# Splitting loaded pairs into a high and a low part: four raw buffers and two low buffers in place of six shared ones

## The reference

```python
# layer 0
h = tanh(concat([X, t], 1) @ W1 + b1);  XB = X @ B.T
x = layernorm(x + h @ W2 + b2 + adj @ XB - rowsum(adj) * XB)
# layer 1: Chebyshev terms, T1 = adj x, T_next = 2 (adj T_curr) - T_prev, three products with adj
x = layernorm(x + x @ w[0] + T1 @ w[1] + T2 @ w[2] + T3 @ w[3] + bias)
# layer 2
z = concat([x, (adj @ x + x) / deg], 1) @ W + b;  out = relu(z) / norm(relu(z))
x = layernorm(x + out)
# layer 3: each row's last 100 nonzeros, weighted by 2**-(number of later nonzeros)
x = layernorm(x + w(adj != 0) @ (x @ weight) + bias)
```

## Time and profile before

| | before |
|---|---|
| median of 3 runs | 3085.93 us |
| the profiled execution | 3082.01 us |
| its span | 3080.2 us |
| TensorE busy | 2934.1 us (95%) |
| VectorE busy | 2831.4 us (92%) |
| ScalarE busy | 2353.7 us (76%) |
| share of the 16 DMA engines taken by SP's queue | 94.6% |
| data moved | 1148.18 MB, 373 GB/s on the mean |
| granted clock, mean | 0.992 |

### The profile page before, as it was taken

One profiled execution on the slowest core, in us unless ns is written; L12 is line 12 of the kernel. 1 busy time (PEld: TensorE's weight loads), 2 busy tenths in 40 slices (PEclk: granted clock), 3 DMA queues, 4 the chain that ended last, 5 costly groups with the idle time before them and its releaser, 6 DMA issues.

```text
span 3080.2 us, 35223 instructions
## 1 busy us (share of the span) xinstructions
PE 2934.1 (95%) x13425; PEld 2164.8 (70%) x13488; DVE 2831.4 (92%) x2407; ACT 2353.7 (76%) x1619; POOL 13.2 (0%) x31
## 2 busy tenths in 40 slices
PE   7999999999999998999989999998889999999998
PEld 6767778787788886888867888776766555555554
DVE  7999988988998889988899988999999999999997
ACT  5787877777777678776777776877777888888887
POOL 0000000000000000000000000000000000000000
PEclk9999999999999999999999999999999999999999
DMA  9999988999999999999999999989999999999996
GB/s 339 388 395 382 387 352 343 369 361 359 370 394 382 377 374 399 387 386 378 377 369 374 382 375 379 377 328 349 373 405 405 359 385 385 377 389 377 388 386 251
DMA packets 159015, 1148.18 MB, mean 373 GB/s; under 512 B 18160, under 2 KB 18336, under 8 KB 19584
## 3 DMA queue, kind: packets, MB, share of 16 engines
q1 hardware_dynamic: 157312, 1143.02, 94.6%
q0 software_dynamic: 1088, 2.48, 0.2%
q10 hardware_dynamic: 448, 0.43, 0.0%
HBM read 1143.75 MB, written 2.10 MB: 372 GB/s over the span
## 4 chain that ended last, share of the span: by engine, by line
PE 66%; DVE 23%; DMA 5%; ACT 3%; issue 2%; ACTq 0%; DVEq 0%
PE ACC L887 26%; DVE lo L626 17%; PE ACC L894 15%; PE ACC L1003 14%; DMA raw<-in_at 5%; PE PST L1017 4%; PE PSF L1017 3%; ACT hi L444 2%; PE PST L910 1%; DVE SV L737 1%; PE PSF L960 1%; DVE M L641 1%; PE PSF L967 0%; PE PSF L983 0%; PE PSF L963 0%
## 5 line engine op out<-in xcount | busy, mean ns | idle before, releaser
L626 DVE TENSOR_TENSOR lo<-raw,hi 128x2048 fp32r<-128x2048 f32 x832 | 1876.4, 2287 | 140.0 <-ACT hi L444 136.2
L444 ACT CAST hi<-raw 128x2048 fp32r<-128x2048 f32 x832 | 1584.7, 1912 | 526.2 <-PE ACC L887 338.4
L887 PE MATMUL ACC<-hi,T 128*128 128x512 f32 x4992 | 1280.6, 393 | 4.5 <-ACT hi L444 2.8
L887 PEld LDWEIGHTS ACC<-hi,T 128*128 128x128 f32 x4992 | 936.0, 189 | 207.6 <-issue 3.9
L894 PE MATMUL ACC<-lo,T 128*128 128x512 f32 x3200 | 887.4, 399 | 103.4 <-DVE lo L626 96.9
L894 PEld LDWEIGHTS ACC<-lo,T 128*128 128x128 f32 x3200 | 589.5, 189 | 298.4 <-DVE lo L626 183.9
L641 DVE SCALAR_TENSOR_TENSOR M<-raw,M 128x512 bf16<-128x512 f32 x1008 | 637.1, 687 | 40.9 <-PE ACC L1003 24.2
L450 ACT ACTIVATE Wf<-ACC,w_bias 128x1024 fp32r<-128x1024 f32 x512 | 568.1, 1114 | 128.5 <-PE ACC L1003 127.9
L1003 PE MATMUL ACC<-M,rank_b 128*128 128x512 bf16 x1969 | 518.3, 382 | 12.2 <-ACT Wf L450 6.7
L1003 PEld LDWEIGHTS ACC<-M,rank_b 128*128 128x128 bf16 x2032 | 158.8, 98 | 266.5 <-issue 131.2
L1017 PE MATMUL PST<-Wf,S 128*128 128x512 f32 x512 | 209.3, 489 | 0.0
(11 more groups left out here) (156 smaller groups left out, 1004.8 us busy)
## 6 DMA issues: line engine op xcount, KB each, us to landing
raw<-in_at SPq DMA_DIRECT2D x1088, 1024.0 KB, 6.8
SV<-in_x_cols SPq DMA_DIRECT2D x8, 256.0 KB, 10.1
out<-O POOLq DMA_DIRECT2D x7, 256.0 KB, 6.9
out<-O ACTq DMA_DIRECT2D x1, 256.0 KB, 2.0
w_sb<-in_w POOLq DMA_DIRECT2D x3, 64.0 KB, 9.6
bias<-in_bias_rows ACTq DMA_DIRECT2D x1, 128.0 KB, 11.8
l1w_sb<-in_l_w POOLq DMA_DIRECT2D x2, 64.0 KB, 8.4
rank_f<-in_rank_mats POOLq DMA_DIRECT2D x1, 128.0 KB, 10.2
```

Source lines behind the costliest of these rows:

```text
L444: nc.scalar.copy(hi[:, c % NH], raw[:, c % NR]).then_inc(hi_done, 1)
L626: tt(lo[:, c % NR], raw[:, c % NR], hi[:, c % NH].bitcast(f32), ALU.subtract).then_inc(lo_done, 1)
L887: ins = mm(acc[:, part], w, hi[:, p.c % NH, s, part], start=p.opens and s == 0 and i == 0, stop=False)
```

## The change

`lo` gets two buffers of its own, and `raw` is cut from six to four; the bytes are the same (six places of 8 KB per partition). A raw pair is given back once the low part has been made: SP waits for `lo_done` of pair c before it loads pair c + 4. VectorE, before it writes the low part of pair c, waits until TensorE is done with the low part of pair c - 2. In the counting pass the raw ring has four places as well.

```diff
-    NR = 6
+    NR = 4
+    NL = 2
...
-    raw, raw_at = place("raw", [P, NR, 2, BLK], f32)
-    lo, _ = place("lo", [P, NR, 2, BLK], f32r, raw_at)
+    raw, _ = place("raw", [P, NR, 2, BLK], f32)
+    lo, _ = place("lo", [P, NL, 2, BLK], f32r)
...
                 if 0 <= before < n_pairs:
-                    sp.wait_ge(pair_done, before + 1)
+                    sp.wait_ge(lo_done, before + 1)
...
                 dve.wait_ge(hi_done, c + 1)
-                tt(lo[:, c % NR], raw[:, c % NR], hi[:, c % NH].bitcast(f32), ALU.subtract).then_inc(lo_done, 1)
+                if c >= NL:
+                    dve.wait_ge(pair_done, c - NL + 1)
+                tt(lo[:, c % NL], raw[:, c % NR], hi[:, c % NH].bitcast(f32), ALU.subtract).then_inc(lo_done, 1)
...
-                        ins = mm(acc[:, part], ws[s][0], lo[:, p.c % NR, s, part], start=False, stop=p.closes and s == 1)
+                        ins = mm(acc[:, part], ws[s][0], lo[:, p.c % NL, s, part], start=False, stop=p.closes and s == 1)
```

## The result

The changed kernel takes 3275.94 us (median of four runs, 3260.26 to 3286.52), the kernel before 3084.29 us in the same comparison: a ratio of 1.062 (95% interval 1.060 to 1.064). Forecast were 3156 us and a range up to 3235. The direction was right; the 70 us that were forecast on top of the kernel before are little more than a third of the 192 measured. The profiled execution has a span of 3258.4 us, 178 more than before.

What follows compares the result with a forecast made beforehand. No single bound: TensorE, VectorE and DMA take turns, sharing the pipeline through the ring. Terms 28 + 8 + 18 + 8 + 9 + 1 = 72 us on 3082 give 3154, plus half of 4 us: 3156 us; range 3105 to 3235.

Steps and rivals of the forecast that it cites:

- Part 1, product 1: Row ends of product 1: the subtraction held up by `comb` makes `fin_a` 5.1 us late; 8 x 3.5 = 28 us.
- Part 1, the other products: Added wait of `split_lo` at row ends: zero in products 2 to 4, 1 us a row or 8 us in product 5.
- Part 2: Shorter raw ring, losses at row ends: 18 us in products 2 to 4, 8 in product 1, 9 in product 5.
- a steady stream fits in four places: Streaming pairs: four places allow a pair each 2.28 us and loads need 2.49, so nothing is lost there.
- almost the full rate: P groups of product 3, 1343 to 1545 us: landing median 5.0 us, cited against the rival of slower loads.
- The one with the loads as the bound throughout: Rival: landings stay at 6.8 or 8.6 us, 384 pairs at about 3.0 us, +135, about 3245 us; chance 0.12.
- fewer loads out make a shorter queue: Against the loads rival: landings of 8.6 us are queue time; median from issue to landing falls from 6.8 towards 5 us.
- No change: Rival: steady sums stream without loss and ends of rows are absorbed; 3083 to 3089 us; chance 0.05.
- faster: Rival: earlier ring release starts the next load 4.4 us earlier in eight rows, 35 us less, 3051 us; chance 0.03.
- The start: Start of the kernel: four loads go out at once and not six; 1 us.
- the counting pass: Counting pass: place reuse after 8.4 us against a landing of 4.8, so four places cover it; 0, upper end 10 us.
- The rule to double-buffer: Skill's advice, read for `lo`: two buffers are enough, the added wait is free everywhere, the sum 36 us less.

Runs made afterwards that it cites:

- low wait alone: Kernel before, six shared places, plus one VectorE wait: the subtraction of pair c waits until TensorE has ended pair c - 2; 3145.82 us, ratio 1.020.
- reach of four alone: Kernel before, six shared places, SP holding back the load of pair c until the subtraction of pair c - 4 (counting pass: its count); 3215.07 us, ratio 1.043.
- loads-alone kernel: Kernel without matmuls and steps, streaming 1 MB loads in sections of 120; with cast and subtraction 2.80 us per load at a reach of four, 2.50 at five.

## Why the prediction was wrong in size

**Part 1, product 1: right.** The same place in the changed kernel (VectorE, then TensorE, timeline):

```profile
321.30 2.29 DVE L629 TENSOR_TENSOR lo<-raw,hi 128x2048 fp32r<-128x2048 f32 x1 [0.16 <-ACT hi L445]
328.61 2.29 DVE L629 TENSOR_TENSOR lo<-raw,hi 128x2048 fp32r<-128x2048 f32 x1 [5.02 <-PE ACC L897]
330.82 0.16 DVE L681 COPY RS<-PSF 128x8 f32<-128x8 f32 x1
...
341.82 4.49 DVE L629 TENSOR_TENSOR lo<-raw,hi 128x2048 fp32r<-128x2048 f32 x2
...
319.31 1.07 PE L897 MATMUL ACC<-lo,T 128*128 128x512 f32 x4
```

Pair 98 ends at 320.38, and `fin_a` starts 10.4 us after it; before it was 296.66 - 291.32 = 5.3. That is 5.1 us late, as forecast. The subtraction after `fin_b` starts 21.4 us after that end, 18.2 before: 3.2 late, forecast 3.3. With the low wait alone TensorE's matmuls with that pair are 3.1 us late. Eight rows at 3.5 us were to give 28; with the low wait alone the seven rows that end before product 1's last one cost between 2.7 and 4.1 us each, and product 1 took 25 us more.

**Part 1, the other products: too low.** Products 2 to 4 were forecast at zero, "`comb` is short (under 2 us) and the row work comes later", and gave 21 us; product 5 at 8 and gave 17. In the row of product 5 that was read, the first wait with the low wait alone is 2.51 us, as forecast (2.5). Then the later waits were to take 1.5 us of it. Instead the delay of TensorE's matmuls grew from 1.7 to 4.9 us within three pairs. Most of that growth is TensorE itself. Before, and then with the low wait alone, the same work reads (the last line is a stretch; columns as in the earlier trace rows):

```profile
2071.44 2.00 PE L983 MATMUL PSF<-l3w_sb,TT 64*128 64x64 f32 x16
2073.37 1.19 PE L887 MATMUL ACC<-hi,T 128*128 128x512 f32 x4
2074.40 1.08 PE L894 MATMUL ACC<-lo,T 128*128 128x512 f32 x4
...
2122.43 1.20 PE L896 MATMUL ACC<-lo,T 128*128 128x512 f32 x4 [1.43 <-DVE lo L628]
2123.56 3.11 PE L985 MATMUL PSF<-l3w_sb,TT 64*128 64x64 f32 x16
2126.59 2.07 PE L889 MATMUL ACC<-hi,T 128*128 128x512 f32 x4
2128.47 1.91 PE L896 MATMUL ACC<-lo,T 128*128 128x512 f32 x4
...
2124.00:2131.00 7.00, 7.00 (x24) 5.94 (x24) 3.89 (x4) 3.48 (x4) 0.00 (x0) 0.51 0.73 269
```

After a pause of 1.43 us for the late subtraction the granted clock is at the lower of its two levels (1.2 GHz in place of 2.4), and the three steps take 2.8 us longer. So a small pause of TensorE can cost more than itself if the clock falls with it; that it was this pause that brought it down isn't shown.

**A term that the prediction left out: TensorE's clock.** The mean granted clock is 0.992 before, 0.987 with the low wait alone, 0.991 with the reach of four alone and 0.984 with the change. With two levels that is about 50, 80, 60 and 105 us at the lower one. Work takes about twice as long there (1.91 us in place of 1.08 above), so the additional time at the lower level can have cost at most half of itself: 16 us of the low wait's 64, 5 us of the reach's 133 and 28 us of the 178 in the change's profile. How much of that it did cost wasn't separated.

**Part 2 is the step that failed.** It was to give 35 us and gave 133, and not only the size was wrong but the mechanism: the cost was to arise at the ends of rows alone, and the loads themselves became slower. (In its sum 8 x 1.2 is 9.6 and not 9, which changes nothing.) The failing sentence is that a steady stream fits in four places, with the loads at 2.49 (or 2.65) us each. The rows read could not carry it: 2.49 us was read where loads had about three in flight (a median of 8.6 us from issue to landing), and it was used for a ring that lets a load be out for 4 x 2.49 - 4.3 = 5.7 us, a little over two loads. The loads-alone kernel gives 2.80 us there. At 2.80 us each the 832 pairs alone make 2330 us, by estimate, of the 2355 that the products took before, so almost nothing is left to hide the work at the ends of rows. The traces bear that floor out: from cast to cast over 20 pairs, half of all such stretches ran below 2.80 us per pair before, and 6% with the reach of four alone. In product 1, in the 137 pairs that lie more than 17 pairs behind a row's end, the reach of four alone cost 31 of that product's 41 us. In products 2 to 4 only 24 pairs each lie so far behind; they took 2.71 to 2.73 us per pair before and 2.78 to 2.89 with the reach of four alone. Most pairs of products 2 to 5 lie nearer to a row's end, and how much of their cost is pace and how much is the smaller store wasn't separated.

**The rows that contradicted it.** From 1343 to 1545 us the median out to landing was 5.0 us at 2.79 us per pair, and I read this as "almost the full rate" with a short queue. TensorE set the pace there, and 5.0 / 2.79 = 1.8 loads were out on the mean. So the row shows that fewer than two loads out can carry 2.79 us per pair; it can't show that they would carry 2.49. In the changed kernel landing stayed at 6.8 us in the median. My reading is that late loads stretch the pace until the ring's reach covers them: 4 x 2.85 - 4.3 = 7.1.

**The rivals.** The one with the loads as the bound throughout (0.12, 3245 us) was nearest. Its argument, that landings stay at 6.8 us, was right by its number. My counter-argument, that fewer loads out make a shorter queue, holds for loads alone (7.45 us in the median with three in flight, 4.96 with two), but I took from it that the pace stays, and it doesn't. That the rival's 135 us are so near to the 133 measured is in part luck: it has 384 pairs slower by 0.35 us each, and the reach of four slowed the P groups too. No change and faster fell: the wait in `split_lo` does hold up the one subtraction that would have to run. The start cost 1 us by pair 15, as forecast, and the counting pass 2 (forecast 0) in the profiled executions. The rule to double-buffer (the Trainium skill, "Trainium Kernel Development and Optimization", Best Practices), taken for `lo`, is not borne out here: two buffers cost 64 us, three cost nothing.

## What to carry to other kernels

Count a ring of load buffers by the time that it lets a load be out (places times pace, less the time from landing to release), and ask that it cover three loads of this size. Where it covers little more than two (5.7 us here), the pace of the loads themselves falls, and no rate read from a deeper ring holds. A cut in buffers is cheap down to an edge and dear beyond it (9 us and then 124; 1 us and then 64), so a hold by one extra wait, in the old kernel, is the way to find the edge before data is moved. A wait added to an instruction of an in-order engine costs what stands behind it: look for the long pauses of the engine waited for. And look at the granted clock where TensorE pauses more often than before.

## What the runs showed of the hardware

With 1 MB loads of 128 partitions on one queue, loads alone: 4.78 us each with one in flight, 2.79 to 2.99 with two, 2.50 with three, 2.49 with four and six. With 512 KB loads: 2.84 us per MB with four in flight, 2.57 with five and six. With three and more in flight nearly all landings are even to some hundredths of a us. With two, most are too, but single ones (13% in one run, 22% in the other) come over 1.3 us late. Of the packets of 8 KB some take over 0.6 us where the usual one takes 0.31: 0.1% with three loads in flight, 1.5% and 2.5% with two, 3.3% and 3.5% at the reach of four, 7.3% with one in flight. Why packets become slow when fewer bytes are queued wasn't found.
